# The first map's bias of a feed-forward: a product with ones on TensorE, or an addition on VectorE

## The reference

```python
    x = x + 0.5 * ffn(layernorm(x))
    x = x + attn(layernorm(x))          # 16 heads of rank 64, softmax over 512 keys
    x = x + 0.5 * ffn(layernorm(x))

    def ffn(h):
        for blk in range(3):
            i0, i1 = 2 * blk, 2 * blk + 1
            y = qlora_linear(h, i0)      # h @ W[i0].T + bias[i0] + (h @ la.T) @ lb.T
            y = layernorm(y) * gamma[blk] + beta[blk]
            y = gelu(y)                  # the exact one
            y = qlora_linear(y, i1)
            h = y + h
        return h
```

## Time and profile before

| | us |
|---|---|
| median of 3 runs | 1027.19 (1026.61 to 1031.52) |
| the profiled execution, its own time | 1026.52 |
| its span, first to last instruction | 1024.7 |
| TensorE busy, mean granted clock | 963.4, 0.979 of full speed |
| VectorE, ScalarE, GpSimd busy | 877.1, 802.6, 784.4 |

### The profile page before, as it was taken

One profiled execution on the slowest core, in us unless ns is written; L12 is line 12 of the kernel. 1 busy time (PEld: TensorE's weight loads), 2 busy tenths in 40 slices (PEclk: granted clock), 3 DMA queues, 4 the chain that ended last, 5 costly groups with the idle time before them and its releaser, 6 DMA issues.

```text
span 1024.7 us, 22051 instructions
## 1 busy us (share of the span) xinstructions
PE 963.4 (94%) x5892; PEld 502.3 (49%) x5892; DVE 877.1 (86%) x1786; ACT 802.6 (78%) x1293; POOL 784.4 (77%) x706
## 2 busy tenths in 40 slices
PE   4895689999999999999999999999999999997897
PEld 4763234444444444444444444444444444444775
DVE  7667898988888889898888888888888888898566
ACT  4885388888888888888888888888888888886874
POOL 2644168888888888888888888888888888886442
PEclk9999699999999999999999999999999999998999
DMA  9000222222222222222222222222222222220002
GB/s 244 1 2 0 51 50 55 62 61 62 63 63 64 64 65 63 64 64 63 63 64 65 63 64 61 61 61 61 61 61 61 61 61 61 61 62 1 1 1 83
DMA packets 71676, 59.03 MB, mean 58 GB/s; under 512 B 11168, under 2 KB 70560, under 8 KB 71648
## 3 DMA queue, kind: packets, MB, share of 16 engines
q1 hardware_dynamic: 71392, 58.31, 24.0%
q10 hardware_dynamic: 256, 0.39, 0.1%
HBM read 6.23 MB, written 2.10 MB: 8 GB/s over the span
## 4 chain that ended last, share of the span: by engine, by line
PE 83%; DVE 10%; ACT 3%; POOL 2%; issue 1%; DMA 1%; SPq 0%; DVEq 0%; POOLq 0%; ACTq 0%
PE ps L1032 11%; PE ps L1034 10%; PE ps L1033 10%; PE ps L1022 10%; PE ps L1023 10%; PE ps L1015 6%; PE ps L1007 3%; PE ps L953 3%; PE ps L1048 3%; PE ps L1044 3%; PE ps L1045 3%; PE ps L1009 3%; PE ps L1008 3%; PE ps L925 2%; DVE stats L654 1%
## 5 line engine op out<-in xcount | busy, mean ns | idle before, releaser
L376 POOL TENSOR_TENSOR p_lo<-work_b,p_hi 128x1024 f16<-128x1024 f32 x256 | 539.8, 2130 | 129.4 <-ACT p_hi L527 129.3
L794 DVE TENSOR_REDUCE mcol<-ps 128x2 f16<-128x1024 f32 x256 | 301.0, 1220 | 0.8 <-PE ps L1015 0.7
L522 ACT ACTIVATE work_b<-ps,exp_scale 128x1024 f32<-128x1024 f32 x256 | 271.6, 1111 | 32.4 <-PE ps L1023 32.3
L527 ACT ACTIVATE p_hi<-work_b 128x1024 f16<-128x1024 f32 x256 | 256.0, 1054 | 0.0
L1022 PE MATMUL ps<-head_ops 128*128 128x512 f16 x512 | 195.1, 381 | 4.1 <-DVE mcol L794 2.0
L1032 PE MATMUL ps<-p_hi,xn_hi 128*128 128x512 f16 x512 | 195.2, 381 | 0.0
L1023 PE MATMUL ps<-head_ops 128*128 128x512 f16 x512 | 195.1, 381 | 0.0
L1033 PE MATMUL ps<-p_hi,xn_lo 128*128 128x512 f16 x512 | 194.4, 380 | 0.0
L1034 PE MATMUL ps<-p_lo,xn_hi 128*128 128x512 f16 x512 | 194.3, 379 | 0.0
L382 POOL TENSOR_TENSOR x<-x,o_sb 128x512 f32 (+1 forms) x128 | 162.7, 1271 | 8.7 <-DVE o_sb L819 8.7
L804 DVE STREAM_TRANSPOSE head_ops<-mcol 32x128 f16<-32x128 f16 x512 | 155.5, 304 | 9.3
(11 more groups left out here) (116 smaller groups left out, 1316.9 us busy)
## 6 DMA issues: line engine op xcount, KB each, us to landing
head_ops<-pair_ops SPq DMA_DIRECT2D x512, 64.0 KB, 2.0
head_ops<-pair_ops SPq DMA_DIRECT2D x128, 128.0 KB, 2.4
x<-x_dram SPq DMA_DIRECT2D x8, 256.0 KB, 5.9
out<-x SPq DMA_DIRECT2D x8, 256.0 KB, 3.0
vo_last<-wvo_dram SPq DMA_DIRECT2D x1, 1024.0 KB, 13.5
qk<-wq_dram SPq DMA_DIRECT2D x1, 512.0 KB, 5.6
qk<-wk_dram SPq DMA_DIRECT2D x1, 512.0 KB, 6.4
scl<-scales_dram ACTq DMA_DIRECT2D x8, 48.0 KB, 5.2
```

What stands on the lines that cost most here:

```text
L376: pool.tensor_tensor(p_lo[:, par, rows, :], p32[:, par, rows, :], p_hi[:, par, rows, :], ALU.subtract).then_inc(plo_done, 1)
L522: nc.scalar.activation(p32[:, par, 2 * a:2 * a + 2, :], s_ps[a], ACT.Exp, scale=exp_scale[:, 0:1]).then_inc(exp_done, 1)
L527: nc.scalar.activation(p_hi[:, par, 2 * a:2 * a + 2, :], p32[:, par, 2 * a:2 * a + 2, :], ACT.Copy).then_inc(phi_done, 1)
L794: nc.vector.tensor_reduce(mcol[:, par, :, t, 0], s_ps[t % 2], AX.X, ALU.max, negate=True).then_inc(max_red, 1)
```

## The change

The bias is no longer part of the product. The rows of `bias_rows` are loaded from memory into all 128 partitions by one DMA on ScalarE's queue; VectorE centres them (one reduction, one small product, three additions). In each step VectorE runs a new operation, `add_bias`, that reads the bank, adds the row and writes fp32 to `work_b` (`zb_ready`). `squares` reads `work_b` and writes its unused squares into the bank, `z_scaled` reads and writes `work_b`. The rows on the old way (means, split, turn, copy, the bf16 identity, two memsets) go.

```diff
@@ GpSimd
-            pool.memset(ones_b[:, :], 1.0)
-            pool.memset(bias_rows[:, :, :], 0.0).then_inc(bias_clear, 1)
@@ ScalarE
-            act.wait_ge(consts, 2)
-            nc.scalar.activation(ident_b[:, :], ident[:, :], ACT.Copy).then_inc(prep_a, 1)
+            act.dma_start(bias_rows[:, :, :], brow_d[0:NL:2, :].partition_broadcast(128)).then_inc(bias_in, 16)
...
             def squares(f, i):
                 for c, b in unit_batches(i):
-                    act.wait_ge(lin1_done, at(f, i, c))
+                    act.wait_ge(zb_ready, at(f, i, c))
                     for t in range(TT):
                         cols = slice(t * D, (t + 1) * D)
-                        ins = nc.scalar.activation(work_b[:, b, cols], bank[b][:, cols], ACT.Square,
+                        ins = nc.scalar.activation(bank[b][:, cols], work_b[:, b, cols], ACT.Square,
                                                    accum_out=sumsq[:, i % UNITS, c * TT + t:c * TT + t + 1])
...
-                if f == 0:
-                    act.wait_ge(bias_clear, 1)
-                    act.wait_ge(bias_turned, 1)
-                    rows = ps[0:3, SG + 3, 0:NB * D].rearrange("p (n d) -> p n d", n=NB)
-                    nc.scalar.activation(bias_rows[0:3, :, :], rows, ACT.Copy).then_inc(bias_ready, 1)
@@ VectorE
-            link(dve, nc.vector.tensor_tensor(bias_c[:, :], bias[:, 0:NL:2], ps[:, SG + 2, 0:NL:2], ALU.subtract))
-            link(dve, nc.vector.tensor_tensor(bias_mid[:, :], bias_c[:, :], bf16_top(bias_c), ALU.subtract))
-            nc.vector.tensor_copy(bias_parts[:, :, 0], bf16_top(bias_c))
-            nc.vector.tensor_copy(bias_parts[:, :, 1], bf16_top(bias_mid))
-            nc.vector.tensor_tensor(bias_parts[:, :, 2], bias_mid[:, :], bf16_top(bias_mid),
-                                    ALU.subtract).then_inc(bias_split, 1)
...
+            dve.wait_ge(bias_in, 16)
+            link(dve, nc.vector.tensor_reduce(row_mean[:, :], bias_rows[:, :, :], AX.X, ALU.add))
+            link(dve, nc.vector.tensor_scalar(row_mean[:, :], row_mean[:, :], -1.0 / D, None, ALU.mult))
+            for n in range(NB):
+                ins = nc.vector.tensor_scalar(bias_rows[:, n, :], bias_rows[:, n, :], row_mean[:, n:n + 1], None,
+                                              ALU.add)
+            link(dve, ins)
+
+            def add_bias(f, i):
+                n = i // UNITS
+                row = bias_rows[:, n, :].rearrange("p (a d) -> p a d", a=1).to_broadcast([128, TT, D])
+                for c, b in unit_batches(i):
+                    dve.wait_ge(lin1_done, at(f, i, c))
+                    nc.vector.tensor_tensor(work_b[:, b, :].rearrange("p (t d) -> p t d", d=D),
+                                            bank[b].rearrange("p (t d) -> p t d", d=D), row,
+                                            ALU.add).then_inc(zb_ready, 1)
...
-                    nc.vector.tensor_tensor(work_b[:, b, :].rearrange(tiles, d=D), bank[b].rearrange(tiles, d=D),
-                                            scale.to_broadcast([128, TT, D]), ALU.mult).then_inc(z_full, 1)
+                    zb = work_b[:, b, :].rearrange(tiles, d=D)
+                    nc.vector.tensor_tensor(zb, zb, scale.to_broadcast([128, TT, D]), ALU.mult).then_inc(z_full, 1)
...
+                    if i < STEPS:
+                        add_bias(f, i)
                     if i >= 3 and i < STEPS + 2:
                         step_h(f, i - 3, 0)
                         step_h(f, i - 3, 1)
@@ TensorE
-                    row = bias_rows[:, n, :].rearrange("p (a d) -> p a d", a=1).to_broadcast([128, TT, D])
-                    nc.tensor.matmul(bank[b].rearrange("p (t d) -> p t d", d=D), ones_b[:, :], row,
-                                     start=True, stop=False)
                     for t in range(TT):
                         ins = nc.tensor.matmul(bank[b][:, t * D:(t + 1) * D], hT[:, b, t * 128:(t + 1) * 128],
-                                               wt[:, 2 * n, :], start=False, stop=(t == TT - 1))
+                                               wt[:, 2 * n, :], start=True, stop=True)
```

More of the change, by code:

```diff
@@ L19, with macaron @@
 AX = mybir.AxisListType
-def macaron(nc, x_d, q_d, k_d, vo_d, qw_d, sc_d, bias_d, la_d, lb_d, gam_d, bet_d, out_d):
+def macaron(nc, x_d, q_d, k_d, vo_d, qw_d, sc_d, bias_d, la_d, lb_d, gam_d, bet_d, brow_d, out_d):
     B, T, D = x_d.shape
@@ L56, in macaron @@
         ident = sb("ident", [128, 128])
-        ident_b = sb("ident_b", [128, 128], BF16)
         mean_mat = sb("mean_mat", [128, 128])
@@ L65, in macaron @@
         bias = sb("bias", [128, NL])
-        bias_c = sb("bias_c", [128, NB])
         gam = sb("gam", [128, NB])
@@ L101, in macaron @@
         u_u = sb("u_u", [128, 2 * TT])
-        ones_b = sb("ones_b", [128, 128], BF16)
-        bias_parts = sb("bias_parts", [128, NB, 3], BF16)
-        bias_mid = sb("bias_mid", [128, NB])
-        bias_rows = sb("bias_rows", [128, NB, D], BF16)
+        bias_rows = sb("bias_rows", [128, NB, D])
+        row_mean = sb("row_mean", [128, NB])
         hT = sb("hT", [128, B, T])
@@ L147, in macaron @@
         prep_pe = sem("prep_pe")
-        bias_clear = sem("bias_clear")
-        bias_split = sem("bias_split")
-        bias_turned = sem("bias_turned")
-        bias_ready = sem("bias_ready")
+        bias_in = sem("bias_in")
+        zb_ready = sem("zb_ready")
         prep_v = sem("prep_v")
@@ L215, in wait_xhat @@
                 eng.wait_ge(xhat_a, (u - 1) * (SG // 2) + c + 1)
-        def bf16_top(t):
-            return t[:, :].bitcast(BF16).rearrange("p (c h) -> p c h", h=2)[:, :, 1]
         def unit_batches(i):
@@ L357, in _ @@
                     fold_last(4 * i + 2)
-            pool.wait_ge(prep_a, 3)
+            pool.wait_ge(prep_a, 2)
             pool.tensor_tensor(w_lo[:, :, :], qk32[:, :, :], w_hi[:, :, :], ALU.subtract).then_inc(prep_p, 1)
-            pool.wait_ge(prep_a, 5)
+            pool.wait_ge(prep_a, 4)
             pool.tensor_tensor(vo_lo[:, :, :], vo32[:, :, :], vo_hi[:, :, 0:D], ALU.subtract).then_inc(prep_p, 1)
@@ L462, in weight_halves @@
                 if i == 10:
-                    act.wait_ge(prep_a, 2)
+                    act.wait_ge(prep_a, 1)
                     for n in range(2):
@@ L886, in _ @@
             pe.wait_ge(consts, 2)
-            nc.tensor.matmul(ps[:, SG + 2, 0:NL], mean_mat[:, :], bias[:, :], start=True, stop=True)
             for n in range(NL):
@@ L904, in pre @@
                     turn(bank[b], lambda t: xhat[:, b * TT + t, :], pre_t)
-            def turn_bias():
-                pe.wait_ge(bias_split, 1)
-                pe.wait_ge(prep_a, 1)
-                for n in range(NB):
-                    ins = nc.tensor.matmul(ps[0:3, SG + 3, n * D:(n + 1) * D], bias_parts[:, n, :], ident_b[:, :],
-                                           start=True, stop=True)
-                ins.then_inc(bias_turned, 1)
             def lin1(f, i):
@@ L967, in ffn @@
                     pre(0, 0)
-                    turn_bias()
                     pe.wait_ge(prep_v, 1)
-                    pe.wait_ge(bias_ready, 1)
                 for i in range(STEPS + 3):
@@ L995, in _ @@
             ffn(0)
-            pe.wait_ge(prep_a, 5)
+            pe.wait_ge(prep_a, 4)
             pe.wait_ge(prep_p, 10)
@@ L1148 @@
         "ln_beta": a["L0_ffn_ln_beta"].T,
+        "bias_rows": a["L0_ffn_biases"],
     }
```

## The result

The changed kernel takes **1057.3 us** (median of 4 runs, 1056.8 to 1059.1) against 1027.0 before: a ratio of 1.0288, 95% interval 1.0257 to 1.0319. The forecast was 1047.3 with a range of 1040 to 1055. The direction is right, the time is over the range.

A forecast was written before the change was run, and what follows sets the result against it. TensorE was taken to bound steady steps (4.81 us), replaced by a VectorE-ScalarE loop of 4.65. From 1026.5 us, +7.3 for the second feed-forward and +13.5 for the first gave 1047.3 us, range 1040 to 1055.

The forecast's parts named there:

- third rival: Both feed-forwards: `lin1(2)` does not move, TensorE's 0.43 us comes off each step it bounds; -5.4, 1021 us; chance 0.03.
- The last two steps stay: End of the first feed-forward: its last two steps keep their time, leaving that stage at +13.5 us.
- rival 2: Squares 0.04 us dearer a pair, 1051 us, plus some 1.2 for `z_scaled` reading two SBUF tensors; chance 0.18.
- The way to the GELU of step 9: First feed-forward, from its start to that GELU: about 13.5 us late.
- The squares' price, +0.02 us a pair: ScalarE's squares in each step: reading SBUF and writing PSUM costs +0.02 us a pair, bounded by -0.02 and +0.04.
- the term for the block of eight: Loop of a steady step: eight pairs of squares take 2.42 us, within a step of 4.65 us.
- The second start, 8.3 us: Start of the second feed-forward: `lin1(2)` 7.6 us late, first GELU at 973.8 against 965.47, 8.3 us late.
- The attention unchanged: Attention between the two feed-forwards: its time does not change.

The follow-up runs named there:

- experiment 12: Kernel before the change, with its bias product left out (first maps' bias missing from the result): 1025.3 us against 1031.0, ratio 0.9944.
- experiment 1: Changed kernel with GpSimd's two long weight products started only after the first feed-forward's last scaling: 1053.8 us, ratio 1.0234.
- experiment 9: Changed kernel with VectorE's sum written back into the PSUM bank; squares and scaling read the bank and write SBUF: 1046.1 us, ratio 1.0153.
- experiment 4: Changed kernel with the squares still reading `work_b` in SBUF but writing idle SBUF instead of the bank: 1058.0 us, one run.
- experiment 6: Changed kernel with squares reading the PSUM bank and writing idle SBUF, still behind the addition (variance leaves the bias out): 1051.3 us, ratio 1.0209.
- experiment 10: experiment 9 plus the first two steps' additions placed ahead of the second half's statistics, in both feed-forwards: 1038.1 us, ratio 1.0067.
- 11: experiment 10 plus VectorE's weight maxima placed ahead of the seeds of their step: 1037.8 us, ratio 1.0066.

## Why the prediction was right in direction and wrong in size

**Right: the mechanism.** The squares wait for VectorE's addition, at each start this pushes ScalarE's scaling and with it `lin1(2)` back, and in the steps a loop takes up what TensorE gives back. `lin1(2)` came at 40.2 us (forecast 40.0) and at 968.1 on the old clock of the second stage (968.0). In the first feed-forward `z_scaled(4)` was at 61.7 (61.1), `z_scaled(5)` at 70.1 (69.4). The work taken off TensorE was worth 5.7 us (experiment 12; 5.4 in the third rival, which needed the start not to move), though not where the rival had it: it counted 1.5 us in the first feed-forward, and the trace shows none there.

**Wrong, step by step**, on the profiled executions (1057.5 against 1047.3, 10.2 us):

1. *"The last two steps stay"*, in the first feed-forward: this is the step that failed, with some 6.1 of the 10.2 us. Up to the GELU of step 9 the stage was 15.1 us late (forecast 13.5). Behind it came 5.05 us of hold (6.33 less 1.28) and 1.6 us of `lin2` at low clock (3.56 less 1.98; the windows show a granted clock of 0.54 from 99.7 to 103.2 behind 2.9 us in which TensorE was idle; before, it was 1.00 at this place behind 2.56 us); 0.5 us came back behind them. Taking the hold away alone gave 3.9 us of the span (experiment 1). I did see that `z_scaled` would read two SBUF tensors, in rival 2 (squares 0.04 us dearer a pair, 1051 us, and some 1.2 more for this), and priced it against Newton's small operations alone. The trace of before showed a VectorE operation on 16 columns that took 2.04 us beside two GpSimd products and ended at 938.39, as they did (938.36); the median of that line is 0.175 us. The large products that GpSimd runs in the same stage stood in the profile of before at 85.82 and 89.85, right beside a scaling (87.46). Of the work that changes its operands I should have looked at every instance and at what GpSimd does beside it, not at the steady one. Experiments 1 and 9 show what the hold needs: the scaling takes 1.28 us with the products elsewhere, and 1.28 beside them with its large source in PSUM.
2. *The way to the GELU of step 9*, +1.6 us. About half of it is a wait that the sum did not have: `weight_scales` waits 0.74 us for TensorE (72.09), whose four products at 65.62 took 3.46 us and not 1.88, at a granted clock of 0.54. So `z_scaled(6)` is 13.4 us late, where the forecast had 12.0; 0.5 us of it was there at `z_scaled(1)` already. In experiment 9 these four take 1.88 us, and `weight_scales` does not wait.
3. *The squares' price, +0.02 us a pair.* Two neighbours in a batch are 0.0425 us further apart than before, since a PSUM destination gives nothing back to an SBUF source (0.29 to 0.30 us apart into PSUM and into SBUF, experiment 4). But the 2.25 us that I started from held a wider distance between the two batches (0.34 us, 962.67 to 963.01), which is gone: eight pairs now take 2.46 us in the chain, against the forecast's 2.42. So the term for the block of eight was right to 0.04 us (a step of 4.69, not 4.65), by two errors that cancel, and that is luck. Over ten steps it makes 0.4 of the 1.6 us. Experiments 6 and 9 show what the form costs against the quick one: with it a step is 4.41 us, and 6 gains 0.8%. On the way to SBUF the source makes 0.04 to 0.05 us: 0.29 to 0.30 (experiment 4) against 0.25 (6), as the copies of the earlier trace rows had it.
4. *The second start, 8.3 us.* It was 9.6 (first GELU at 996.95, less 21.9, against 965.47): `lin1(2)` at a granted clock of 0.50 took 3.62 us, where it takes 2.05 at 1.00 (1018.31). In the kernel before, the twelve transposes at 957.57 had a granted clock of 0.51, behind 3.7 us of idle time and four others. I had allowed the doubling in words ("up to twice that after a gap") and taken about 2.4 in the sum.
5. *The attention unchanged*: +0.6 us, which is within the 3 us by which it differs from trace to trace.

Together 7.7 (6.1 + 1.6) + 0.6 + 1.7 = 10.0 for the first stage, the attention and the second, and 0.1 in what lies around the span.

**The whole account**, for the 30 us, by the ratios and, in brackets, by the two stages in the traces: +14 (11.5) are where the sum is put and what reads it from there (experiment 9: hold and squares' form, with TensorE's products at 65.62); +9 (8.0) are VectorE's order at the two starts (10 against 9); the rest is 7 (10.7). The two readings differ because the kernel before took 2.5 to 4.5 us more on the later chips (medians of 1029.0 to 1031.0) than in its trace (1026.5). Where the rest lies is shown: in experiment 10 the second stage is level with the kernel before (69.1 against 69.3), and all of it, 11.0 us, is in the first. That it comes from the longer path from `lin1` over the addition to the squares is argued, not shown. That 9 ends near the forecast (1046 and 1047) is partly chance, since its steps are 4.41 us and not 4.65.

**Open.** Why only the way from PSUM to SBUF is quick for ScalarE (0.25 us against 0.28 to 0.30). Where 10 still loses time in the first feed-forward: its first scaling is 5.9 us late, its fifth 8.2, its last 10.3 (97.75 us against 87.46); of what lies there the start and the place of the maxima were tried. Why TensorE's clock fell to 0.54 at 65.62 and 99.71 and stayed at 1.00 at the same places before. No version with the addition on VectorE beat the kernel before; the best, 10 and 11, are 0.7% slower by the ratios.

## What to carry to other kernels

A step moved from one engine to another changes more than two busy times: list who now waits for it (the loop through the squares), what stands in front of it on its new engine at the start of a stage, and what form the neighbours' operands take. Keep a result that VectorE and ScalarE read next in PSUM where it fits: here that alone was worth 11 to 14 of 30 us. And when an operation gets two SBUF sources, look through the whole trace for long GpSimd products that it may run beside (here 1.28 us became 6.33), in every instance and not in the steady step only. To compare versions that ran on different chips, compare their stages too, and look at a stage that no edit touches for the noise.

## What the runs showed of the hardware that was not expected

- VectorE and GpSimd hold each other in both directions. A scaling of 1.28 us took 6.33 and 7.90 beside two GpSimd products of 4 us, and 2.33 (36.57) beside two GpSimd sums of 128 x 256; in experiment 9, out of PSUM, it took 1.28 and 1.29 at these places. The 6.33 are 2.00 and 4.41 us for the two instructions, the 7.90 of experiment 6 are 3.57 and 4.40: the first ends soon after GpSimd's first product, the second soon after its second. The other way, GpSimd's small operation took 0.51 and 0.53 us beside a scaling out of SBUF, against 0.20 beside one out of PSUM (experiment 9, 1004.76 above):

```profile
1005.97 0.51 POOL L327 TENSOR_TENSOR u_t<-u_rstd 128x8 f32<-128x8 f32 x1 [0.73 <-DVE u_rstd L700]
1006.56 0.53 POOL L328 TENSOR_TENSOR u_u<-u_t,u_var 128x8 f32<-128x8 f32 x1
1007.17 0.20 POOL L329 TENSOR_SCALAR u_t<-u_u 128x8 f32<-128x8 f32 x1
```

- ScalarE's squares of 128 columns with a sum are 0.25 us apart from PSUM to SBUF (experiment 6), and 0.28 to 0.30 in the other three forms.
- VectorE's addition of 128 x 512 takes about as long into PSUM (0.686 us in the steady steps of experiment 9) as into SBUF (0.677 in the changed kernel).
- The busy share misleads in a loop: from 1001 to 1038 us TensorE is busy for 36.1 of 37 us at full clock in the changed kernel, and yet the chain of that stretch runs through ScalarE's squares (53%) and VectorE's scaling and addition (39%), and a step of 4.38 us of TensorE work takes 4.69.
